# Vision-transformer block on one core: a token's place in the tiles goes from c*99+p to 2p+c

## The chip, the cores and the metric

The kernel runs on one core of a Trainium2 chip. The metric is the device time of one execution in microseconds, the median of three runs: 1737.85 us before the change (1737.76 to 1738.62). TensorE (PE), VectorE (DVE), ScalarE (ACT), GpSimd (POOL) and SyncE (SP) each run a program of their own and meet at semaphores. SP computes nothing: it issues most of the transfers, in order, and a transfer that has to wait for a semaphore holds up those behind it.

## The reference, cut to what matters

128 images of 224x224x3 become 196 patch tokens each (with four shifted copies), one class token stands ahead of them, and one block of attention and a quantised linear layer follow. All is float32.

```python
h = _L0_tok_ref(x, L0_tok_W, L0_tok_b)                   # (128, 196, 192)
h = jnp.concatenate([broadcast(cls_tok), h], axis=1)     # (128, 197, 192)
h = h + _L0_attn_ref(_layernorm(h), Wq, Wk, Wv, Wo, ...) # 6 heads of 32, softmax over 197 keys
h = h + _L0_ffn_ref(_layernorm(h), weight_t, bias)       # round to int8 steps, 192x192 product
return h
```

Attention mixes the tokens of an image without regard to their order; the other steps treat each token for itself. So the order in which tokens lie in a tile is free, as long as loads and store agree on it and the padding is left out.

## The kernel before

It has two stages. The first (`build_tokens`, up to about 420 us) embeds the patches, measures each token for the layer norm and stores two scratch tensors in DRAM, `h_dram` (the tokens, the residual) and `xn_dram` (the normalised tokens), each 128 x 198 x 192: 197 tokens and one row of zeros as padding (TP = 198 = 2 x TC, TC = 99).

The second stage (`build_attention`) takes the images one after the other. An image's 198 rows lie in a tile as 99 partitions by 2 halves by 192 columns. Before, half c of partition p holds token c*99+p; the padding, row 197, is partition 98 of half 1, which the value product (`kk = NTOK - TC`) and the padding's score row leave out.

Each engine's program is written out by hand in `step(i)`: at step i it works on image i+5 (transposing the normalised tokens, `f`), on the pair of images two or three ahead (query and key projections, `p`), on i+1 (scores and row maxima, `a`), i (transposed scores and exponentials, `b`), i-1 (values, `c`), i-2 (output projection and residual, `e`), i-3 (quantising, `g`) and i-4 (linear layer and store, `k`). Steps -5 to 11 and 120 to 131 are written out, and 108 steps in between run as a loop of six steps (MOD = 6): 18 passes, with a jump back between them on every engine.

What SP issues in one step, in its order: the two loads of normalised tokens for image i+7 (`load_xn`, lines 768 to 770: all 192 columns, and columns 128 to 191 a second time, into `xn_in`, which has 256 columns per half); the copies from SBUF to SBUF that stack high and low parts of queries and keys for the score product (`stack`, line 762: in odd steps nine into `q_st` and `k_st`, in even steps three into `k_st`), behind waits for ACT's and DVE's parts; the store of image i-4 (lines 825 and 826: 99 rows of half 0, 98 rows of half 1); the load of the residual of image i-1 (`h_in`, line 830); and, behind a wait for ACT, the row maxima of image i+1 into `q_st` (line 752). TensorE waits before the first score product of an image (`score`, lines 903 to 908) for all stacked copies of its pair. VectorE adds the residual in line 1257 after a wait for line 830's load, and writes `y` in line 1239 after a wait for the store of the image two before.

Of the kernel before, what the change touches and what calls it, by code (L numbers as in the profile page):

```python
# [21 lines left out]
NTOK = G * G + 1  # L22
TP = NTOK + 1
TC = TP // 2
# [602 lines left out]
def build_attention(nc, s):  # L627
# [17 lines left out]
    def tile(name, shape, dt=F32):  # L645
        return sb(name, shape, dt, attention)
# [25 lines left out]
    h_in = tile("h_in", [TC, NS, 2, D])  # L672
# [6 lines left out]
    y = tile("y", [TC, NS, 2, D])  # L679
# [16 lines left out]
    y_stored = [sem(f"y_stored{i}") for i in range(MOD)]  # L696
# [25 lines left out]
    def images(eng, step):  # L722

        first, last = 2 * MOD, B - 8
        assert first % MOD == last % MOD == 0
        for i in range(-5, first):
            step(At(0, i, MOD))
        with eng.Fori(first // MOD, last // MOD) as k:
            for r in range(MOD):
                step(At(k, r, MOD))  # L730
        for i in range(last, B + 4):
            step(At(0, i, MOD))

    def pair_of(i):

        return i.plus(3 if i.r % 2 else 2)

    def leads(n):

        return n.fixed and 0 <= n.n < 2  # L740

    def stack_one(eng, image, dst, row, heads, src):

        eng.dma_start(dst[row * HD:(row + 1) * HD, 0, heads[0]:heads[1], image, :].bitcast(F32),
                      src[:, image * TP:(image + 1) * TP].bitcast(F32))\
            .then_inc(stacked[0] if image else first_stacked, 16)

    def store_max_rows(eng, a):
        if a.fixed and a.n == 0:
            eng.wait_ge(no_score_made, 1)  # L750
        eng.wait_ge(mrow_done, a.count(1, 1))
        eng.dma_start(q_st[ST:ST + 2, a.pair, :, a.two, :].bitcast(F32), max_rows[:, a.two, :].bitcast(F32))\
            .then_inc(max_landed[a.slot], 16)
# [4 lines left out]
    with nc.Block() as block:  # L758
        @block.sync
        def _(sp):  # L760
            def stack(p, dst, row, heads, src):
                sp.dma_start(dst[row * HD:(row + 1) * HD, p.pair, heads[0]:heads[1], :, :].bitcast(F32),
                             src.bitcast(F32)).then_inc(stacked[p.pair], 16)

            def load_xn(n):
                if n.reuses(NX):
                    sp.wait_ge(xt_done, n.count(1, 1 - NX))
                by_chunk = xn_dram[n.n].rearrange("(c p) d -> p c d", p=TC)
                sp.dma_start(xn_in[:, n.slot % NX, :, 0:D], by_chunk).then_inc(xn_landed[n.slot], 16)
                sp.dma_start(xn_in[:, n.slot % NX, :, D:DA + 2 * DB], by_chunk[:, :, DA:D]).then_inc(xn_landed[n.slot], 16)  # L770

            def step(i):
                f, p, a, c, k, ahead = i.plus(5), pair_of(i), i.plus(1), i.plus(-1), i.plus(-4), i.plus(7)
                if i.fixed and i.n == -5:
                    load_xn(f)
                    load_xn(f.plus(1))
                if ahead.within(B):
                    load_xn(ahead)
                q_first, q_last, k_first = (0, 4), (4, H), (0, SPLIT)
                q_rows, k_rows = slice(0, SPLIT * HD), slice(SPLIT * HD, BLOCK)  # L780
                if leads(p) and i.r % 2:
                    sp.wait_ge(qkhi_done, p.pair_count(3, 1))
                    stack_one(sp, 0, q_st, 0, q_first, qk_hi[:, 0, :])
                    stack_one(sp, 0, q_st, 1, q_first, qk_hi[:, 0, :])
                    sp.wait_ge(qklo_done, p.pair_count(3, 1))
                    stack_one(sp, 0, q_st, 2, q_first, qk_lo[:, 0, :])
                    sp.wait_ge(qkhi_done, p.pair_count(3, 2))
                    stack_one(sp, 0, q_st, 0, q_last, qk_hi[q_rows, 1, :])
                    stack_one(sp, 0, q_st, 1, q_last, qk_hi[q_rows, 1, :])
                    sp.wait_ge(qklo_done, p.pair_count(3, 2))  # L790
                    stack_one(sp, 0, q_st, 2, q_last, qk_lo[q_rows, 1, :])
                elif leads(p):
                    stack_one(sp, 1, q_st, 0, q_first, qk_hi[:, 0, :])
                    stack_one(sp, 1, q_st, 1, q_first, qk_hi[:, 0, :])
                    stack_one(sp, 1, q_st, 2, q_first, qk_lo[:, 0, :])
                    stack_one(sp, 1, q_st, 0, q_last, qk_hi[q_rows, 1, :])
                    stack_one(sp, 1, q_st, 1, q_last, qk_hi[q_rows, 1, :])
                    stack_one(sp, 1, q_st, 2, q_last, qk_lo[q_rows, 1, :])
                elif p.within(B) and i.r % 2:

                    sp.wait_ge(qkhi_done, p.pair_count(3, 1))
                    stack(p, q_st, 0, q_first, qk_hi[:, 0, :])
                    stack(p, q_st, 1, q_first, qk_hi[:, 0, :])
                    sp.wait_ge(qklo_done, p.pair_count(3, 1))
                    stack(p, q_st, 2, q_first, qk_lo[:, 0, :])
                    sp.wait_ge(qkhi_done, p.pair_count(3, 2))
                    stack(p, q_st, 0, q_last, qk_hi[q_rows, 1, :])
                    stack(p, q_st, 1, q_last, qk_hi[q_rows, 1, :])  # L810
                    stack(p, k_st, 0, k_first, qk_hi[k_rows, 1, :])
                    stack(p, k_st, 2, k_first, qk_hi[k_rows, 1, :])
                    sp.wait_ge(qklo_done, p.pair_count(3, 2))
                    stack(p, q_st, 2, q_last, qk_lo[q_rows, 1, :])
                    stack(p, k_st, 1, k_first, qk_lo[k_rows, 1, :])
                elif p.within(B):
                    k_last = (SPLIT, H)
                    sp.wait_ge(qkhi_done, p.pair_count(3, 3))
                    stack(p, k_st, 0, k_last, qk_hi[:, 2, :])
                    stack(p, k_st, 2, k_last, qk_hi[:, 2, :])  # L820
                    sp.wait_ge(qklo_done, p.pair_count(3, 3))
                    stack(p, k_st, 1, k_last, qk_lo[:, 2, :])
                if k.within(B):
                    sp.wait_ge(y_done, k.count(1, 1))
                    sp.dma_start(out[k.n, 0:TC, :], y[:, k.two, 0, :]).then_inc(y_stored[k.slot], 16)
                    sp.dma_start(out[k.n, TC:NTOK, :], y[0:NTOK - TC, k.two, 1, :]).then_inc(y_stored[k.slot], 16)
                if c.within(B):
                    if c.reuses(NS):
                        sp.wait_ge(h1_done, c.count(1, 1 - NS))
                    sp.dma_start(h_in[:, c.two, :, :], h_dram[c.n].rearrange("(c p) d -> p c d", p=TC))\  # L830
                        .then_inc(h_landed[c.slot], 16)
                if a.within(B) and not leads(a):
                    store_max_rows(sp, a)

            sp.dma_start(h_dram[:, (G - 1) * G + 1:NTOK, :], h_t[:, LAST, 0:G, :]).then_inc(last_row_stored, 16)
            sp.wait_ge(last_row_xn, G - EARLY)
            sp.dma_start(xn_dram[:, (G - 1) * G + 1 + EARLY:NTOK, :], xn_t[:, EARLY:G, :]).then_inc(last_row_stored, 16)
            sp.wait_ge(last_row_stored, 32)
            sp.wait_ge(pads_stored, 32)
            sp.wait_ge(cls_landed, 32)  # L840
            for p in range(2):
                sp.wait_ge(h_stored[p], 16 * (G // 2 - p))
            sp.wait_ge(xn_stored, 16 * G)
            sp.wait_ge(early_stored, 16)
            images(sp, step)
            for n in range(B - MOD, B):
                sp.wait_ge(y_stored[n % MOD], 32 * (n // MOD + 1))
# [585 lines left out]
```

## Time and profile before

| | before |
|---|---|
| median of 3 runs (lowest to highest) | 1737.85 us (1737.76 to 1738.62) |
| span of the profiled execution | 1736.1 us |
| busy: TensorE, its weight loads, VectorE | 95%, 87%, 85% of the span |
| busy: GpSimd, ScalarE | 53%, 44% |
| DMA queue of SP's copies | 65.4% of 16 engines' span, 204690 packets |

The profile gives one execution, seen by the hardware profiler; its span runs from the first to the last instruction. Its own time outside the span is not recorded, so the median of the runs stands beside it: 1.75 us lie around the span. A DMA packet is one piece moved by one of the 16 DMA engines. An entry "issue" in a list of waits is idle time for which the profile shows no releaser.

### The profile page before, as it was taken

What the parts mean: (1) busy time and instruction counts of PE and PEld (TensorE: products, weight loads), DVE (VectorE), ACT (ScalarE), POOL (GpSimd) and SP (SyncE); (2) the same over time, 40 slices, a digit from 0 to 9 for tenths busy, and PEclk for the clock granted to TensorE, in tenths of its full rate; (3) what the DMA queues carried; (4) which work ended last, traced back from release to release, by engine and by line L of the source; (5) the groups of instructions that cost most, each with busy time, mean ns of one, the idle gap of its engine ahead of it and who ended that gap; (6) DMA issues with size and microseconds to landing.
All of it is one profiled execution on the core that took longest, in us unless ns stands there. A gap on an engine that the chain in (4) does not pass through costs nothing.

```text
span 1736.1 us, 53274 instructions
## 1 busy us (share of the span) xinstructions
PE 1655.0 (95%) x16368; PEld 1504.7 (87%) x16368; DVE 1471.9 (85%) x3906; ACT 759.4 (44%) x1751; POOL 925.9 (53%) x1911
## 2 busy tenths in 40 slices
PE   4999999996699999999999999999999999999996
PEld 4999999996588888888888888888888888888884
DVE  7888888895388988888888888888888888888885
ACT  2000000001265555556565555655556555555653
POOL 3353544536055655555555565556555555555555
PEclk9999999998699999999999999999999999999998
DMA  9999999973777778787887878877787878878771
GB/s 299 265 306 297 314 290 308 314 257 143 123 140 151 142 146 146 148 147 138 148 149 149 145 139 147 150 146 143 143 147 146 150 138 147 147 150 145 139 119 33
DMA packets 216158, 303.66 MB, mean 175 GB/s; under 512 B 47776, under 2 KB 205011, under 8 KB 205988
## 3 DMA queue, kind: packets, MB, share of 16 engines
q1 hardware_dynamic: 204690, 227.17, 65.4%
q10 hardware_dynamic: 7426, 39.47, 7.8%
q0 software_dynamic: 3984, 36.28, 5.3%
q8 instruction: 32, 0.52, 0.1%
q14 instruction: 26, 0.21, 0.0%
HBM read 126.54 MB, written 58.29 MB: 106 GB/s over the span
## 4 chain that ended last, share of the span: by engine, by line
PE 50%; DVE 8%; POOL 7%; issue 7%; DMA 2%; SPq 1%; ACT 0%; ACTq 0%; POOLq 0%; DVEq 0%
PE bank L874 9%; PE o_bank L932 8%; PE bank L922 6%; PE bank L908 6%; PE bank L895 5%; PE bank L883 5%; PE o_bank L855 3%; PE o_bank L951 2%; PE bank L855 2%; PE o_bank L960 2%; POOL ln L163 2%; DVE neg_max L1193 2%; PE bank L1007 2%; DMA k_st<-qk_lo 2%; POOL qx L1369 2%
## 5 line engine op out<-in xcount | busy, mean ns | idle before, releaser
L1093 ACT ACTIVATE probs<-bank 99x396 f32<-99x396 f32 x768 | 381.8, 497 | 217.7 <-PE bank L922 217.4
L1336 POOL TENSOR_TENSOR key_sum<-probs 99x396 f32<-99x396 f32 x256 | 227.4, 888 | 433.5 <-ACT probs L1093 284.5
L1193 DVE TENSOR_REDUCE neg_max<-bank 99x2 f32<-99x394 f32 x768 | 419.4, 560 | 16.4 <-PE bank L908 12.3
L340 PE MATMUL bank<-e_t,xt 128*128 128x192 f32 x2352 | 389.0, 329 | 25.2 <-DVE xt L448 21.5
L340 PEld LDWEIGHTS bank<-e_t,xt 128*128 128x128 f32 x2352 | 387.5, 192 | 26.4 <-DVE xt L448 26.2
L922 PE MATMUL bank<-q_st,k_st 99*99 99x198 f32 x1536 | 280.6, 264 | 5.7 <-DMA q_st<-max_rows 2.9
L908 PE MATMUL bank<-k_st,q_st 96*99 96x198 f32 x1536 | 275.6, 275 | 10.1 <-DMA k_st<-qk_lo 4.1
L448 DVE STREAM_TRANSPOSE xt<-x_t 128x256 f32<-128x256 f32 x588 | 214.9, 416 | 46.0 <-PE bank L340 44.6
L922 PEld LDWEIGHTS bank<-q_st,k_st 99*99 99x99 f32 x1536 | 208.0, 167 | 50.5 <-issue 42.5
L908 PEld LDWEIGHTS bank<-k_st,q_st 96*99 96x99 f32 x1536 | 193.3, 167 | 26.8 <-issue 12.6
L932 PE MATMUL o_bank<-probs,vals 99*32 99x198 f32 (+1 forms) x3072 | 199.0, 337 | 0.0
L1087 ACT ACTIVATE o_t<-o_bank 128x396 f32<-128x396 f32 x128 | 64.1, 501 | 234.9 <-PE o_bank L951 234.9
L932 PEld LDWEIGHTS o_bank<-probs,vals 99*32 99x32 f32 (+1 forms) x3072 | 113.6, 110 | 47.3 <-ACT probs L1093 0.2
L951 PE MATMUL o_bank<-key_sum,pick 99*32 99x198 f32 x1536 | 151.9, 332 | 0.0
L1369 POOL TENSOR_SCALAR qx<-h,ln 99x192 f32<-99x192 f32 x256 | 126.4, 501 | 40.1 <-POOL ln L163 40.1
L1348 POOL TENSOR_TENSOR hb<-h,ffn_bias 99x384 f32<-99x384 f32 x128 | 129.4, 1011 | 3.7 <-DVE h L1257 3.7
L349 ACT ACTIVATE ffn_w_bf<-ffn_raw 96x384 bf16<-96x384 int8 x1 | 0.5, 522 | 294.8 <-DVE xt L448 294.8
L163 POOL TENSOR_TENSOR ln<-ln,minus_half 99x2 f32<-99x2 f32 x128 | 116.0, 906 | 23.1 <-POOL ln L162 23.1
L1210 DVE TENSOR_TENSOR qk_lo<-bank,qk_hi 128x396 fp32r<-128x396 f32 x192 | 108.3, 564 | 19.4 <-ACT qk_hi L1102 18.4
L895 PE MATMUL bank<-wo_hi,a_mix 128*99 128x192 f32 x512 | 120.3, 253 | 0.0
L895 PE MATMUL bank<-wo_lo,a_mix 128*99 128x192 f32 x512 | 120.2, 253 | 0.0
L1102 ACT ACTIVATE qk_hi<-bank 128x396 fp32r<-128x396 f32 x192 | 96.1, 501 | 49.9 <-PE bank L874 43.2
(134 smaller groups left out, 3593.0 us busy)
## 6 DMA issues: line engine op xcount, KB each, us to landing
x_t<-in_x_dram SPq DMA_DIRECT2D x26, 1344.0 KB, 21.9
x_t<-in_x_dram ACTq DMA_DIRECT2D x26, 1344.0 KB, 23.1
q_st<-qk_hi SPq DMA_DIRECT2D x126, 198.0 KB, 4.4
k_st<-qk_hi SPq DMA_DIRECT2D x126, 198.0 KB, 4.4
xn_in<-xn_scratch SPq DMA_DIRECT2D x128, 148.5 KB
h_in<-h_scratch SPq DMA_DIRECT2D x128, 148.5 KB
h_scratch<-h_t POOLq DMA_DIRECT2D x13, 1344.0 KB, 17.2
xn_scratch<-xn_t POOLq DMA_DIRECT2D x13, 1344.0 KB, 8.0
```

The source lines that it names most:

```text
L340: last = pe.matmul(token_bank(p)[:, 0:D], xt[:, p, c // 3, c % 3, :], e_t[:, row_kind(t), col, c // 3, c % 3, :], start=c == 0, stop=c == 5)
L448: last = nc.vector.transpose(xt[:, p, :, c, :].rearrange("p m (g b) -> p g m b", b=32), pix[:, c])
L874: last = pe.matmul(wide(bank, BLOCK), weights[:, Q:K + 1, :].rearrange("p w n -> p (w n)")[:, cols], inputs, start=i == 0, stop=i == len(p ...
L895: last = pe.matmul(bank[0:TC, c * D:(c + 1) * D], inputs, weights, start=i == 0, stop=i == len(pairs) - 1)
L908: last = pe.matmul(S_BANK[h % 2][0:TC, c * TP:(c + 1) * TP], q_st[0:ST, n.pair, h, n.two, c * TC:(c + 1) * TC], k_st[0:ST, n.pair, h, n.tw ...
L922: last = pe.matmul(T_BANK[0:TC, c * TP:(c + 1) * TP], k_st[:, n.pair, h, n.two, c * TC:(c + 1) * TC], q_st[:, n.pair, h, n.two, :], start= ...
L932: pe.matmul(o_bank[at % 4 * HD:(at % 4 + 1) * HD, 0, col:col + TP], vals[0:kk, n.two, kc, h, :], probs[0:kk, n.two, h, kc, :], start=kc == ...
L951: last = pe.matmul(o_bank[to:to + HD, 0, TP:2 * TP], pick[:, j, :], key_sum[:, n.two, HEAD_AT[side * HG + j], :], start=j == 0, stop=j == ...
L1093: nc.scalar.activation(probs[:, n.two, h, :, :], wide(T_BANK, TC), ACT.Exp).then_inc(exp_done, 1)
L1193: nc.vector.tensor_reduce(out=neg_max[:, n.two, :, h], in_=wide(S_BANK[h % 2], TC)[:, :, 0:NTOK], axis=AX_X, op=ALU.max, negate=True).then ...
L1336: nc.gpsimd.tensor_tensor(key_sum[:, b.two, heads, :], probs[:, b.two, heads, 0, :], probs[:, b.two, heads, 1, :], ALU.add).then_inc(pool_ ...
L1369: nc.gpsimd.tensor_scalar(qx[:, e.two, cc, :], h1[:, e.two, cc, :], v[7][:, cc:cc + 1], v[6][:, cc:cc + 1], ALU.add, ALU.mult).then_inc(ln ...
```

## The change

Half c of partition p now holds token 2p+c. Row 197, the padding, stays at partition 98 of half 1. The two tokens of a partition are neighbours in DRAM: 2 x 768 = 1536 bytes. The load of the residual and the store therefore name one run of 384 columns per partition; token 196 (partition 98, half 0) has a store of its own. The load of normalised tokens reads neighbouring rows, into a tile whose halves are 256 columns apart.

```diff
-                by_chunk = xn_dram[n.n].rearrange("(c p) d -> p c d", p=TC)
+                by_chunk = xn_dram[n.n].rearrange("(p c) d -> p c d", c=2)
...
-                    sp.dma_start(out[k.n, 0:TC, :], y[:, k.two, 0, :]).then_inc(y_stored[k.slot], 16)
-                    sp.dma_start(out[k.n, TC:NTOK, :], y[0:NTOK - TC, k.two, 1, :]).then_inc(y_stored[k.slot], 16)
+                    sp.dma_start(out[k.n, 0:NTOK - 1, :].rearrange("(p c) d -> p c d", c=2), y[0:TC - 1, k.two, :, :])\
+                        .then_inc(y_stored[k.slot], 16)
+                    sp.dma_start(out[k.n, NTOK - 1:NTOK, :], y[TC - 1:TC, k.two, 0, :]).then_inc(y_stored[k.slot], 16)
...
-                    sp.dma_start(h_in[:, c.two, :, :], h_dram[c.n].rearrange("(c p) d -> p c d", p=TC))\
+                    sp.dma_start(h_in[:, c.two, :, :], h_dram[c.n].rearrange("(p c) d -> p c d", c=2))\
                         .then_inc(h_landed[c.slot], 16)
```

No instruction changes its place. SP's program of before, from the k_st copies of an even step to the first copy of the odd step behind it (partitions x pieces x columns of the destination; `out_dram` is the result):

```order
L762 DMA k_st<-qk_lo 32x4x396
L825 DMA out_dram<-y 99x192
L826 DMA out_dram<-y 98x192
L830 DMA h_in<-h_scratch 99x2x192
L752 DMA q_st<-max_rows 2x6x198
L769 DMA xn_in<-xn_scratch 99x2x192
L770 DMA xn_in<-xn_scratch 99x2x64
L762 DMA q_st<-qk_hi 32x4x396 x2
```

Here the residual's load and both stores name runs of 192 columns. The same place in the changed kernel:

```order
L762 DMA k_st<-qk_lo 32x4x396
L825 DMA out_dram<-y 98x384
L827 DMA out_dram<-y 1x192
L831 DMA h_in<-h_scratch 99x384
L752 DMA q_st<-max_rows 2x6x198
L769 DMA xn_in<-xn_scratch 99x2x192
L770 DMA xn_in<-xn_scratch 99x2x64
L762 DMA q_st<-qk_hi 32x4x396 x2
```

The two stores and the residual's load have other shapes; the loads of normalised tokens keep theirs, and the order is the same.

## Rows read from the trace of the kernel before

**Rows 1.** Windows: us, busy us of PE, PEld, DVE, ACT, POOL, clock, DMA share, GB/s
```profile
430.00:485.00 55.00, 39.34 (x261) 33.83 (x262) 23.23 (x55) 16.76 (x37) 3.55 (x4) 0.66 0.69 123
485.00:1650.00 1165.00, 1154.69 (x13011) 1025.07 (x13011) 1033.05 (x2674) 685.49 (x1604) 680.99 (x1428) 1.00 0.79 146
```

**Rows 2.** Head of the page
```profile
span 1736.1 us, 53274 instructions
```

**Rows 3.** Waits of PEld from 485 to 1650 us: us, times, longest
```profile
PEld bank L908 <- issue: 12.6, 33, 0.5
PEld bank L908 <- DMA k_st<-qk_lo: 0.4, 1, 0.4
```

**Rows 4.** Timeline of PEld at 871 and 881 us: start, us, idle before
```profile
871.75 0.34 PEld L908 LDWEIGHTS bank<-k_st,q_st 96*99 96x99 f32 x3 [0.46 <-issue]
...
880.99 0.44 PEld L908 LDWEIGHTS bank<-k_st,q_st 96*99 96x99 f32 x4 [0.19 <-issue]
```

**Rows 5.** Timeline of SP, 869.8 to 876.4 us: start, us of issue
```profile
870.40 0.35 SPq L826 DMA_DIRECT2D out_dram<-y  x1
870.94 0.33 SPq L830 DMA_DIRECT2D h_in<-h_scratch  x1
872.08 0.67 SPq L752 DMA_DIRECT2D q_st<-max_rows  x1
873.46 0.33 SPq L769 DMA_DIRECT2D xn_in<-xn_scratch  x1
873.97 0.30 SPq L770 DMA_DIRECT2D xn_in<-xn_scratch  x1
874.39 1.26 SPq L762 DMA_DIRECT2D k_st<-qk_hi  x2
875.70 0.61 SPq L762 DMA_DIRECT2D k_st<-qk_lo  x1
```

**Rows 6.** DMA view, 873.9 to 875.4 us, while the token load runs
```profile
DMA packets 202, 0.14 MB, mean 97 GB/s; under 512 B 19, under 2 KB 202, under 8 KB 202
q1 hardware_dynamic: 202, 0.14, 40.8%
```

**Rows 7.** DMA view, 1733.5 to 1736.1 us, the last store
```profile
DMA packets 222, 0.15 MB, mean 58 GB/s; under 512 B 25, under 2 KB 222, under 8 KB 222
q1 hardware_dynamic: 222, 0.15, 20.1%
```

**Rows 8.** DMA view, 421.9 to 424.7 us, a store of 4608-byte rows
```profile
DMA packets 144, 0.59 MB, mean 211 GB/s; under 512 B 16, under 2 KB 16, under 8 KB 144
q1 hardware_dynamic: 144, 0.59, 52.4%
```

**Rows 9.** DMA view, 870 to 876 us: busy tenths in 40 slices
```profile
DMA  9999999999999999877777651000059016777789
```

**Rows 10.** Waits of all engines over the span
```profile
DVE h L1257 <- PE bank L895: 23.1, 79, 0.9
```

**Rows 11.** Waits of SP over the span
```profile
SPq L752 <- ACT max_rows L1087: 303.6, 124, 5.4
SPq L847 <- DMA out_dram<-y: 1.2, 1, 1.2
```

**Rows 12.** Views of two one-row loads: ns of issue min/median/max
```profile
L358 ACTq DMA_DIRECT2D an_row<-in_L_attn_anchors_dram x1: 228/228/228, 1.5 to 1.5; - x1
...
L360 ACTq DMA_DIRECT2D lam_row<-in_L_attn_lam_dram x1: 266/266/266, 1.8 to 1.8; - x1
```

**Rows 13.** Timeline of SP at the end
```profile
1733.58 0.30 SPq L825 DMA_DIRECT2D out_dram<-y  x1
1733.91 0.36 SPq L826 DMA_DIRECT2D out_dram<-y  x1
```

**Rows 14.** Page, sections 2 and 3
```profile
DMA packets 216158, 303.66 MB, mean 175 GB/s; under 512 B 47776, under 2 KB 205011, under 8 KB 205988
...
q1 hardware_dynamic: 204690, 227.17, 65.4%
```

## The prediction

> **What bounds the kernel now.** I read the windows first: from 485 to 1650 us, where nearly all images are worked on, TensorE is busy 1154.69 of 1165 us at a granted clock of 1.00, the level of 2.4 GHz [rows 1]. That leaves 10.3 us of idle time in two thirds of the span [rows 2], and the change leaves every TensorE instruction as it is. In the same rows the DMA engines are busy 0.79, so the second question is whether some transfer lands late for TensorE. The waits of its weight loads answer that [rows 3]: of the waits before the first score matmul (L908), 0.4 us are put down to the DMA into k_st and 12.6 us, in 33 waits, to "issue".
>
> Two rows of one loop turn tell these 33 apart [rows 4]. The wait of 0.46 us at 871.75 comes where TensorE's own program jumps back; with 18 passes there are 17 such turns, 17 x 0.46 = 7.8 us. The other 16 waits hold 12.6 - 7.8 = 4.8 us. Of these 880.99 is one: SP issued the last k_st piece at 875.70 [rows 5] and the score matmul started 5.3 us later, 0.19 us late. It happens once a pass, because SP's jump back (872.08 + 0.67 to 873.46) delays the token load and with it the three k_st copies behind it. So all that a faster or slower DMA could give or take in the body hangs on how soon the k_st copies of a pass's first image land: at most 4.8 + 0.4 = 5.2 us to win.
>
> **The change, part by part.**
>
> *Load of normalised tokens (xn_in).* The destination keeps 256 columns per half, so a partition's two halves do not join: the program's row stays 99x2x192, with the second copy at 99x2x64. The same 198 + 198 pieces move, from neighbouring rows of DRAM instead of rows 99 apart. This is the only one of the three that stands ahead of the k_st copies on SP at the place that counts [rows 5]. Its cost after is not shown by any row, so I bound it. In the stretch in which its large pieces run, 40.8% x 16 x 1.5 us = 9.8 us for 202 packets, 48 ns each [rows 6]; the pieces of the last store, the same 768 bytes, cost 20.1% x 16 x 2.6 = 8.4 us for 222 packets, 38 ns [rows 7]. If the new order brought the load down to 38 ns, it would be done 198 x 10 / 16 = 0.13 us sooner, a little more if fewer than 16 engines share it; I call that 0.2 us. If it brought the pieces up to 70 ns (my estimate below for a piece of twice the size, the dearest near row), it would be 198 x 22 / 16 = 0.27 us later. I take zero, the same pieces at the same price.
>
> *Load of the residual (h_in) and the store.* 198 pieces become 99, and 99 + 98 become 98 + 1. The price of a joined piece is an estimate from two rows: 768 bytes cost at most 8.4 us / 197 = 42 ns if the 25 small packets are free [rows 7], and 4608 bytes 52.4% x 16 x 2.8 / 128 = 183 ns [rows 8]. The line through both gives 70 ns for 1536 bytes, so a pair saves 84 - 70 = 14 ns, and an image 197 x 14 = 2.8 us of engine time, 0.17 us on each of 16 engines. Nothing waits for that in the body. The DMA engines stand idle between the end of store, residual and maxima and the start of the token load: four slices of 0.15 us at about 873.8 to 874.4 read 0 [rows 9]. What ends sooner ahead of that gap only widens it. VectorE's addition of the residual waits, where it waits, for TensorE (23.1 us, 79 times), and the list of waits has no entry that names the transfer [rows 10]. So both edits count zero in the body; if that cover were gone, 0.17 us an image over some 120 images, 20 us, would be the most, but TensorE's idle time of 10.3 us caps it and the 5.2 us above are the only part of it that waits for transfers. SP's wait for the maxima (L752, 303.6 us in 124 waits [rows 11]) also hides the issue time of the single-row store: 0.35 us for the row it replaces (870.40 [rows 5]), 0.23 and 0.27 us for two one-row copies of the start [rows 12]; before the maxima at 872.08 SP has 872.08 - 871.27 = 0.8 us [rows 5].
>
> The Trainium skill, "DMA: Bandwidth & Descriptors" (Specifications), names 512 bytes as the size from which a transfer runs at line rate, and by that joining 768-byte pieces gains nothing, 0 instead of 14 ns a pair. The rows disagree in part: 768 bytes in 42 ns is 18 bytes per ns, 4608 in 183 ns is 25. By either the body's sum is zero.
>
> *The end.* After VectorE's last result SP issues the two stores at 1733.58 and 1733.91 [rows 13] and waits 1.2 us for them [rows 11]. Engine time falls from 8.4 us to 98 x 70 + 42 ns = 6.9 us, and the second transfer is one piece instead of 98. I take 0.2 us off; it can't be over 1.2 us, and a single row that lands late costs at most about the 0.35 us of an issue.
>
> The same page ("Why a DMA increments its semaphore by 16 and not by 1") says that a copy from SP runs on the largest number of engines up to 16 that divides the outer size on both sides, each posting one completion. The 25 small packets beside 197 pieces agree: 11 for 99 rows and 14 for 98. By it the new store uses 14 engines and the single row one, with 7 or 8 pieces on the fullest instead of 16, and the token load stays on 11; the 0.2 us stands.
>
> *The start of the attention stage.* From 430 to 485 us TensorE is busy 39.3 of 55 us [rows 1]; the token loads there keep their pieces. I take zero, with half a us to either side.
>
> **Sum.** Body 0, start 0, end -0.2: the span goes from 1736.1 [rows 2] to 1735.9 us. The median of the runs shown, 1737.85 us, is 1.75 us above the span of the profiled execution; I keep that: 1737.6 us. 0.2% of it, about what a measurement here tells from no change, is 3.5 us.
>
> **Rivals.** (1) Faster: the token load gets cheaper with neighbouring rows, the k_st copies land sooner, and the 16 late starts shrink. For it: the load's pieces do cost 10 ns more than the store's. Against it: a 0.2 us gain takes at most 16 x 0.2 = 3.2 us, which is 1734.4 us; only the whole 5.2 us, 1732.4 us, is clearly beyond 3.5 us. I set this case at 1733.9 us, chance 0.09. (2) Slower: the token load gets dearer, because its engines now read a closer stretch of DRAM and get in each other's way; k_st then lands later in the first image of each of 18 passes, where nothing is left to hide it. At 0.27 us later, 18 x 0.27 = 4.9 us, 1742.5 us; it decides from 3.5 / 18 = 0.19 us on. Against it: the load's pieces and bytes are the same, and the first 768-byte pieces are slow before as well. Chance 0.07. (3) The single row disturbs: a store of one row per image that lands late, or start and end shift by more than I count; the y buffer is needed again only two images later, so it is worth a us or two, 1739 us, chance 0.06. (4) My forecast, which includes that one of the three transfers doesn't get larger pieces at all: 1737.6 us, chance 0.78, its own range 1736.5 to 1738.7.
>
> Faster by over 0.2%: 0.09; slower by over 0.2%: 0.07; within: 0.84. The range goes from 1734.4 (all of a 0.2 us earlier landing) to 1740.5 us (a landing 0.16 us later, 18 x 0.16 = 2.9 us), and leaves out about 0.14.
>
> **What would show it.** Right: DMA packets fall by 128 x (197 + 10) = 26,496; the queue of SP's copies falls from 65.4% by 128 x 2.8 / (16 x 1736) = 1.3 points [rows 14]; TensorE's idle time from 485 to 1650 us stays within 3 us of 10.3; the 33 waits before L908 stay at about 12.6 us. Wrong: that sum moves by several us with the copies into k_st landing other than 5.3 us after issue; a wait of VectorE for h_in, or of SP for a slot of its queue; matmuls of other length.

## The result and the profile after

The changed kernel takes 1803.11 us (median of four runs, 1800.19 to 1807.71) against 1737.8 us before (four runs too): the ratio is 1.0383 with a 95% interval from 1.0366 to 1.0399. The time is 65 us longer, far outside the predicted range.

The head of the profile after, and the windows (columns as in [rows 1]):

```profile
span 1800.9 us, 53274 instructions
```
```profile
485.00:1650.00 1165.00, 1100.42 (x12270) 969.23 (x12269) 976.27 (x2526) 647.88 (x1517) 649.37 (x1349) 1.00 0.77 138
```

In the same 1165 us TensorE is busy 1100.42 us, 54.3 less than in [rows 1], at the same granted clock of 1.00 (2.4 GHz). The instructions are as many as in [rows 2]. So TensorE waits; its waits in this stretch (us, times, longest) say for what. First its products before and after, then its weight loads after, to be held against the 12.6 us in 33 waits of [rows 3]:

```profile
PE bank L908 <- DMA k_st<-qk_lo: 0.8, 4, 0.3
```
```profile
PE bank L909 <- DMA k_st<-qk_lo: 54.8, 55, 1.5
PEld bank L909 <- issue: 73.0, 70, 1.8
```

L909 is L908 of before, the first score product. Over the whole span the page puts it so, before and after (busy us, mean ns, then idle before it and what ended most of that):

```profile
L908 PE MATMUL bank<-k_st,q_st 96*99 96x198 f32 x1536 | 275.6, 275 | 10.1 <-DMA k_st<-qk_lo 4.1
```
```profile
L909 PE MATMUL bank<-k_st,q_st 96*99 96x198 f32 x1536 | 276.1, 275 | 66.3 <-DMA k_st<-qk_lo 60.9
```

The product itself is as long as before (275 ns). Before, the idle time ahead of it was 10.1 us over the span; the 56.2 us more are most of the 64.8 us by which the span grew. The place is the one the prediction watched, the landing of the k_st copies, but late in 55 steps of the window, about 1 us each on average; the window has 56 even steps. To see why they land late, SP's timeline in an even step at a loop turn (start, us of issue), the counterpart of [rows 5]:

```profile
953.58 0.32 SPq L831 DMA_DIRECT2D h_in<-h_scratch  x1
954.45 0.73 SPq L752 DMA_DIRECT2D q_st<-max_rows  x1
955.93 0.97 SPq L769 DMA_DIRECT2D xn_in<-xn_scratch  x1
957.09 0.84 SPq L770 DMA_DIRECT2D xn_in<-xn_scratch  x1
958.06 1.28 SPq L762 DMA_DIRECT2D k_st<-qk_hi  x2
959.38 0.60 SPq L762 DMA_DIRECT2D k_st<-qk_lo  x1
```

Every issue but two is about as long as before. The two token loads take 0.97 and 0.84 us of SP where they took 0.33 and 0.30. From the maxima to the last k_st copy it is 954.45 to 959.38, 4.93 us; in [rows 5] it was 872.08 to 875.70, 3.62 us. What follows, in the chain of waits and in the timelines of TensorE's product and weight load:

```profile
959.38 5.41 DMA k_st<-qk_lo
```
```profile
964.91 0.60 PE L909 MATMUL bank<-k_st,q_st 96*99 96x198 f32 x4 [1.48 <-DMA k_st<-qk_lo]
```
```profile
964.91 0.43 PEld L909 LDWEIGHTS bank<-k_st,q_st 96*99 96x99 f32 x4 [1.72 <-issue]
```

The product starts 5.5 us after the copy's issue, before 5.3 us, so the landing is nearly what it was; but the copy is issued 1.3 us later, and the weight load waits 1.72 us in place of 0.19 [rows 4]. That the long issue holds for all 128 images is seen in the view of the tile, before and after (ns of issue, min/median/max; first and last start):

```profile
L769 SPq DMA_DIRECT2D xn_in<-xn_scratch x128: 292/337/619, 424.8 to 1637.9; - x128
L770 SPq DMA_DIRECT2D xn_in<-xn_scratch x128: 297/297/730, 425.1 to 1638.3; - x128
```
```profile
L769 SPq DMA_DIRECT2D xn_in<-xn_scratch x128: 811/936/1040, 421.4 to 1702.6; - x128
L770 SPq DMA_DIRECT2D xn_in<-xn_scratch x128: 811/866/1273, 422.5 to 1703.6; - x128
```

By the medians (337 and 297 ns before) the two loads together take 1.17 us more of SP. The program as built shows what changed in them. Source and destination of the first load, as [step in elements, count] for each dimension:

```
before  source [192, 99] [19008, 2] [1, 192]   destination [1536, 99] [256, 2] [1, 192]   marked
after   source [192, 198] [1, 1] [1, 192]      destination [1536, 99] [256, 2] [1, 192]   not marked
```

Rows 2p and 2p+1 for all p lie at one distance, so the source is written as one dimension of 198 rows; the destination, with a hole of 64 columns between its 192s, stays 99 x 2. The lists of instructions ahead of the prediction give the destination's shape alone, and there nothing had changed. The "mark" is one that the built program calls "precooked"; in the attention stage every copy of SP whose two sides have the same counts carries it, and none whose sides differ. By the medians of the traces, the marked copies there issue in 0.23 to 0.43 us (h_in, the stores, the token load of before), the others in 0.59 to 0.94 us (stack copies, described as 128 rows against 32 x 4, or 64 against 32 x 2; the maxima, 12 against 2 x 6; the token load of after). Mark and like description always go together here, so no run tells them apart.

The rest went as the change says. Packets, against [rows 14]:

```profile
DMA packets 189662, 303.65 MB, mean 169 GB/s; under 512 B 46496, under 2 KB 178515, under 8 KB 179492
...
q1 hardware_dynamic: 178194, 227.17, 64.6%
```

### The profile page after: what moved, and what is told of

Read it like the earlier page. It is cut to its first block, busy times and chain, and to the rows that moved or that the text cites. A ratio compares the mean times of both kernels' runs of the same rounds, so it can differ in the third digit from the quotient of the medians.

```text
span 1800.9 us, 53274 instructions
## 1 busy us (share of the span) xinstructions
PE 1660.1 (92%) x16368; PEld 1502.5 (83%) x16368; DVE 1473.2 (82%) x3906; ACT 759.7 (42%) x1751; POOL 933.3 (52%) x1911
## 2 busy tenths in 40 slices
DMA packets 189662, 303.65 MB, mean 169 GB/s; under 512 B 46496, under 2 KB 178515, under 8 KB 179492
## 3 DMA queue, kind: packets, MB, share of 16 engines
q1 hardware_dynamic: 178194, 227.17, 64.6%
## 4 chain that ended last, share of the span: by engine, by line
PE 36%; DMA 18%; SPq 13%; issue 4%; DVE 2%; POOL 2%; ACT 1%; ACTq 1%; POOLq 0%; DVEq 0%
DMA k_st<-qk_lo 17%; PE bank L875 7%; PE o_bank L933 5%; PE bank L909 5%; PE bank L923 5%; SPq L762 4%; SPq L769 3%; PE bank L884 3%; SPq L770 3%; PE bank L896 3%; SPq L752 2%; PE bank L856 2%; PE o_bank L856 2%; PE o_bank L961 2%; PE o_bank L952 1%
## 5 line engine op out<-in xcount | busy, mean ns | idle before, releaser
L909 PE MATMUL bank<-k_st,q_st 96*99 96x198 f32 x1536 | 276.1, 275 | 66.3 <-DMA k_st<-qk_lo 60.9
L909 PEld LDWEIGHTS bank<-k_st,q_st 96*99 96x99 f32 x1536 | 193.5, 167 | 91.5 <-issue 75.2
L1370 POOL TENSOR_SCALAR qx<-h,ln 99x192 f32<-99x192 f32 x256 | 143.1, 566 | 40.1 <-POOL ln L163 40.1
L1201 DVE TENSOR_TENSOR key_sum<-probs 99x396 f32<-99x396 f32 x128 | 74.5, 582 | 62.2 <-ACT probs L1094 62.2
```

Source lines behind the costliest of these rows:

```text
L909: last = pe.matmul(S_BANK[h % 2][0:TC, c * TP:(c + 1) * TP], q_st[0:ST, n.pair, h, n.two, c * TC:(c + 1) * TC], k_st[0:ST, n.pair, h, n.tw ...
L1370: nc.gpsimd.tensor_scalar(qx[:, e.two, cc, :], h1[:, e.two, cc, :], v[7][:, cc:cc + 1], v[6][:, cc:cc + 1], ALU.add, ALU.mult).then_inc(ln ...
```

## The experiments

The first four ask which part does it, and whether it is the place on SP. First the changed kernel with the token load in its old order (residual and store stay changed):

```diff
-                by_chunk = xn_dram[n.n].rearrange("(p c) d -> p c d", c=2)
+                by_chunk = xn_dram[n.n].rearrange("(c p) d -> p c d", p=TC)
```

> The changed kernel with the load of normalised tokens alone put back to rows 99 apart (residual and store keep the new order, so the residual is added to other tokens). Theory 1 (issue): after the change SP takes 0.94 + 0.87 us instead of 0.34 + 0.30 us to issue the two token loads, because the source now reads as 198 rows and the destination as 99 x 2; the k_st copies behind them leave 1.2 us later and TensorE waits. With the old source the issue is back at 0.34 + 0.30 us and the time at that of before, 1735 to 1740 us. Theory 2 (joined pieces): the 1536-byte pieces or the single-row store hold up SP's ring; the time stays at 1795 to 1805 us.

Measured: 1737.17 us, ratio 1.0009 [0.9999, 1.0018]. Its tile view and its page:

```profile
L769 SPq DMA_DIRECT2D xn_in<-xn_scratch x128: 292/337/622, 424.9 to 1639.1; - x128
```
```profile
L909 PE MATMUL bank<-k_st,q_st 96*99 96x198 f32 x1536 | 275.7, 275 | 9.8 <-issue 3.9
```

So the larger pieces of the residual and the store, with the single-row store, come to between 0 and 3 us of loss, which can't be told from nothing. The converse, the kernel before with the token load alone in the new order:

```diff
-                by_chunk = xn_dram[n.n].rearrange("(c p) d -> p c d", p=TC)
+                by_chunk = xn_dram[n.n].rearrange("(p c) d -> p c d", c=2)
```

> The kernel before with the new order in the load of normalised tokens alone (residual and store in the old order, so the residual is added to other tokens). Theory 1 (issue): 1798 to 1808 us, with 0.9 us of issue for each of the two loads. Theory 2 (joined pieces): 1735 to 1740 us. Theory 3 (the reads of neighbouring rows are slow on the DMA engines): also about 1803 us, but with the load's packets dearer than the 48 ns of before and the issue unchanged.

Measured: 1795.63 us, 1.0341 [1.0324, 1.0358]. The long issue and the wait come with this one line, and with them 60 of the 65 us; its interval does not meet that of the whole change, and where the last few us come from is not shown:

```profile
L769 SPq DMA_DIRECT2D xn_in<-xn_scratch x128: 811/927/1036, 425.0 to 1698.0; - x128
```
```profile
L908 PE MATMUL bank<-k_st,q_st 96*99 96x198 f32 x1536 | 276.5, 275 | 58.0 <-DMA k_st<-qk_lo 52.8
```

Next, the changed kernel with the token load moved ahead of the wait for the maxima, so that the k_st copies no longer stand behind it in SP's program:

```diff
-                if ahead.within(B):
-                    load_xn(ahead)
                 q_first, q_last, k_first = (0, 4), (4, H), (0, SPLIT)
...
                         .then_inc(h_landed[c.slot], 16)
+                if ahead.within(B):
+                    load_xn(ahead)
                 if a.within(B) and not leads(a):
```

> The changed kernel with SP's two token loads moved from the head of a step to behind the residual's load, ahead of the row maxima, where SP waits for ScalarE anyway. Same loads, same issue time. Theory 1 (issue): the k_st copies no longer stand behind the loads, so the 60 us go: 1733 to 1742 us, although the issue stays at 0.9 us each. Theory 3 (slow reads): the loads still run on the same DMA engines, right ahead of the copies, and at most half of the loss goes: 1765 us or more.

> The kernel before with the same move of the token loads. Theory 1 (issue): the copies of every image leave about 1 us sooner than before, and the up to 5.2 us of late starts that the trace of before shows ahead of the first score product go: 1731 to 1736 us. If the copies' landing is set by the DMA engines and not by when SP issues them: 1736 to 1740 us, no change.

The second is the same move in the kernel before. Measured: 1750.2 us, 1.0089 [1.0072, 1.0106], and 1742.4 us, 1.0036 [1.0022, 1.005]; both are above what was expected. The loads of the moved changed kernel still take 0.93 and 0.88 us, yet most of the 65 us is gone: length of issue costs only where something late stands behind it. What is left goes at least in part with something that I had not expected: in both, TensorE waits for the maxima. The waits of its weight loads, moved changed kernel first, then the moved kernel before:

```profile
PEld bank L923 <- DMA q_st<-max_rows: 23.2, 59, 1.4
```
```profile
PEld bank L922 <- DMA q_st<-max_rows: 39.7, 59, 2.4
```

The same view of the kernel before, where the token load comes behind the maxima, and then a piece of the chain of waits in the moved kernel before (start, us):

```profile
PEld bank L922 <- DMA q_st<-max_rows: 0.6, 2, 0.3
```
```profile
1289.76 3.85 DMA q_st<-max_rows
```

ScalarE had ended the maxima at 1289.70, SP issued them at once, and their 9.3 KB landed 3.85 us after the issue. So here a small copy issued right behind the token load lands late, and the expectation for the kernel before failed on that; that the load's packets ahead of it are the reason is argued, not shown. In the moved changed kernel it is the issue again (ScalarE, then SP):

```profile
957.33 0.31 ACT L1088 ACTIVATE max_rows<-o_bank 12x198 fp32r<-12x198 f32 x1
```
```profile
957.96 0.87 SPq L770 DMA_DIRECT2D xn_in<-xn_scratch  x1
958.94 0.72 SPq L752 DMA_DIRECT2D q_st<-max_rows  x1
```

The maxima were ready at 957.64, but SP was at the token loads until 958.83 and issued them 1.3 us late; TensorE's wait for them ends at 961.10, 2.2 us after that issue. The k_st copies of this kernel, too, are still late in 18 steps of the window, 6.1 us in all.

Is it SP's time, or the order of the rows in DRAM? One kernel adds SP time without touching the token load, by two copies of 12 pieces of 64 bytes, described as 12 against 2 x 6:

```diff
...
+                for j in range(2):
+                    few = xn_dram[n.n, 0:12, 16 * j:16 * j + 16].rearrange("(p c) d -> p c d", c=6)
+                    sp.dma_start(spare[:, n.slot % NX, j, :, :], few).then_inc(spare_landed[n.slot], 16)
...
```

> The kernel before, all rows in the old order, with two tiny copies more behind each pair of token loads: 12 pieces of 64 bytes each from the token scratch into a spare tile, source 12 rows, destination 2 x 6. They move next to nothing and cost SP an estimated 0.6 to 0.7 us of issue each, since the maxima's copy of the same shape takes 0.67 us. Theory 1 (issue time of SP ahead of the k_st copies): 1.2 to 1.6 us of delay per image, 1795 to 1825 us. Theory 3 (slow reads) and theory 2 (joined pieces), which need the data: 1735 to 1740 us.

Measured: 1855.6 us, 1.0689 [1.0674, 1.0705]. The tile of the two copies, and TensorE's waits:

```profile
L778 SPq DMA_DIRECT2D spare<-xn_scratch x256: 610/650/789, 425.4 to 1755.4; - x128
```
```profile
PE bank L917 <- DMA k_st<-qk_lo: 79.2, 54, 2.0
```

Each copy moves 768 bytes and holds SP for 0.65 us, twice as long as the first token load in the old order with its 198 pieces of 768 bytes. That confirms the place and the kind of the cost. The size was missed: 118 us, above the range of the expectation. Part of the excess is TensorE's clock. A piece of its timeline, and two stretches right behind it (columns as in [rows 1]):

```profile
920.34 0.97 PE L917 MATMUL bank<-k_st,q_st 96*99 96x198 f32 x4 [1.91 <-DMA k_st<-qk_lo]
```
```profile
920.40:923.80 3.40, 3.40 (x13) 3.35 (x14) 1.04 (x2) 0.67 (x2) 1.89 (x4) 0.50 0.24 62
923.80:929.00 5.20, 5.20 (x69) 4.40 (x69) 4.22 (x10) 2.06 (x5) 0.00 (x0) 1.00 0.85 128
```

After a wait of 1.91 us for k_st the granted clock is 0.50, the level of 1.2 GHz, for 3.4 us. The window has 13 such stretches, each behind a wait of 1.6 to 1.9 us for k_st; the steps that hold them take 13.4 to 13.7 us, while loop turns without one take 11.9 to 12.2. At about 1.5 us each they are some 20 of the 118 us. (The changed kernel has two such stretches in the window, 3 us by the same estimate.)

Half the dose, the kernel before with only the first of the two loads in the new order:

```diff
+                near = xn_dram[n.n].rearrange("(p c) d -> p c d", c=2)
-                sp.dma_start(xn_in[:, n.slot % NX, :, 0:D], by_chunk).then_inc(xn_landed[n.slot], 16)
+                sp.dma_start(xn_in[:, n.slot % NX, :, 0:D], near).then_inc(xn_landed[n.slot], 16)
```

> The kernel before with only the first of the two token loads in the new order; the 64-column copy keeps the old one (so the doubled columns belong to other tokens). Theory 1 (issue): one load at 0.93 us, the other at 0.30 us, the copies leave 0.6 us later instead of 1.2 us. The trace of before has about 0.4 us of room in two of three even steps and none at a loop turn, so less than half of the loss: 1750 to 1770 us. A cost per byte or per piece read from neighbouring rows would be three quarters of the loss (768 of 1024 bytes a row), about 1780 us.

Measured: 1767.16 us, 1.0172 [1.0157, 1.0187], half the loss for one long issue (the second load's median is 374 ns):

```profile
L770 SPq DMA_DIRECT2D xn_in<-xn_scratch x128: 836/931/1034, 424.5 to 1667.2; - x128
```

Then near rows with a source that can't be joined: partition p reads rows p and p+1 (so most rows are read twice, others not at all).

```diff
+                rows_in = xn_dram[n.n].rearrange("(c p) d -> p c d", p=TC)
+                by_chunk = bass.AP(rows_in.tensor, rows_in.offset, [[D, TC], [D, 2], [1, D]])
```

> The kernel before with token loads that read rows p and p+1 into partition p (neighbouring rows, so most tokens are read twice and the upper half of an image not at all), which keeps the source at 99 x 2 as the destination is. Theory 1 (issue, from the differing description of the two sides): issue stays at 0.34 + 0.30 us, 1735 to 1740 us. Theory 3 (reads of neighbouring rows are slow): 1780 us or more.

Measured: 1736.86 us, 1.0001 [0.9992, 1.001], with an issue as in the old order (the second load's median is 297 ns):

```profile
L770 SPq DMA_DIRECT2D xn_in<-xn_scratch x128: 292/337/556, 424.0 to 1637.7; - x128
```

And the changed kernel's own rows 2p+c with sides that agree, by one pair of copies for each half:

```diff
+                for c in range(2):
+                    sp.dma_start(xn_in[:, n.slot % NX, c, 0:D], by_chunk[:, c, :]).then_inc(xn_landed[n.slot], 16)
+                    sp.dma_start(xn_in[:, n.slot % NX, c, D:DA + 2 * DB], by_chunk[:, c, DA:D]).then_inc(xn_landed[n.slot], 16)
...
-                    pe.wait_ge(xn_landed[f.slot], f.landed(32))
+                    pe.wait_ge(xn_landed[f.slot], f.landed(64))
```

> The changed kernel, with its token load split by halves into four copies, 99 x 192 and 99 x 64 for each half: the same rows 2p+c to the same places, but source and destination described alike. Theory (SP's issue is long where the two sides are described with different counts): each copy issues in 0.30 to 0.35 us, so four of them with 0.2 us between take 1.9 us against 2.0 us for the two long ones and 0.8 us before; the k_st copies leave 1.1 us later than before, 64 even steps lose 0.7 to 0.8 us each, and the time is about 1785 us (1775 to 1797). Rival (rows at the new distance are what takes SP longer): each of the four takes 0.5 us or more, 2.6 us in all, and the time is 1830 us or more.

Measured: 1789.91 us, 1.0301 [1.0285, 1.0317]. The issue of each copy, and the wait that is left:

```profile
L770 SPq DMA_DIRECT2D xn_in<-xn_scratch x256: 292/319/609, 423.3 to 1689.2; - x128
L771 SPq DMA_DIRECT2D xn_in<-xn_scratch x256: 296/297/1120, 423.7 to 1689.6; - x128
```
```profile
PE bank L910 <- DMA k_st<-qk_lo: 43.9, 56, 1.4
```

The same rows, each copy taking every second one, issue in 0.32 and 0.30 us once both sides are described alike; the copies carry the mark. The rival, that the distance of rows costs SP its time, is out by these two runs. But four issues with their gaps hold the k_st copies up nearly as long as two long ones, and the time says so.

Last, a version that takes the token loads off this path: loads for two images together in even steps, ahead of the wait for the maxima, and none in odd steps, where k_st copies follow (line numbers of the kernel before; the changed kernel got the same edit).

```diff
-                if ahead.within(B):
+                if i.fixed and i.n == -5:
                     load_xn(ahead)
...
+                if i.r % 2 == 0:
+                    for n in (ahead, ahead.plus(1)):
+                        if n.within(B):
+                            load_xn(n)
```

> The kernel before, rows in the old order, with the token loads of two images issued together in even steps, between the residual's load and the maxima, where SP waits 4 us for ScalarE, and none in odd steps. The k_st and q_st copies then stand directly behind the maxima in both kinds of step, and in odd steps nothing new stands ahead of the maxima. If the late starts before the first score product come from SP's issue order alone: the 5.2 us of them go, 1730 to 1734 us (0.1 to 0.3% under before). If the maxima of even steps land late behind two token loads, as those of odd steps did with one load ahead: 1738 to 1745 us.

> The changed kernel with the token loads of two images issued together in even steps, ahead of the maxima, and none in odd steps. Issue stays at about 0.93 + 0.87 us a load pair, so four loads take some 4.2 us with the gaps; between the residual's load and the maxima of an even step the version of before with this order has 950.57 to 955.28 us, 4.7 us. Theory 1 (issue): the long issue is hidden in that wait, all of the loss goes, and the time is that of the old row order with the same placing, 1727 to 1735 us. If the maxima are pushed past the room they have: 1740 us or more. If the joined pieces are worth anything once issue is out of the way, it comes out under 1727 us.

> The kernel before with the token loads of two images issued together in even steps, ahead of the wait for the maxima, again, now on one chip with the same edit of the changed kernel. Theory: 1730 us, ratio 0.996; TensorE's waits for k_st copies gone but for the 17 loop turns.

> The changed kernel with the same pairing, on the same chip. Theory: with the k_st copies no longer behind the token loads, issue time is all hidden and larger pieces are worth nothing: the same as the paired kernel before within 0.1% (1730 us). Rival: the joined load still costs something in the even steps, where four issues of 0.9 us stand ahead of the maxima: 4 us more, 1734 us, with waits for q_st<-max_rows in the list.

Measured for the kernel before with paired loads: 1729.91 us, 0.9957 [0.9942, 0.9971], and on another chip 1732.44 us, 0.9972 [0.9961, 0.9984]. For the changed kernel with paired loads: 1734.37 us, 0.9993 [0.9983, 1.0002], and beside the second run of the former 1733.44 us, 0.9976 [0.9967, 0.9985]. In the one comparison on the same chip the two paired versions can't be told apart: taken off the path, the long issues cost nothing and the joined pieces bring nothing that shows above some 3 us. (The first two runs, each on a chip of its own against the kernel before there, differ by 0.4%; why is not known.) SP in the paired kernel before, second run:

```profile
949.38 0.33 SPq L830 DMA_DIRECT2D h_in<-h_scratch  x1
949.91 0.33 SPq L769 DMA_DIRECT2D xn_in<-xn_scratch  x1
950.43 0.30 SPq L770 DMA_DIRECT2D xn_in<-xn_scratch  x1
950.92 0.30 SPq L769 DMA_DIRECT2D xn_in<-xn_scratch  x1
951.40 0.30 SPq L770 DMA_DIRECT2D xn_in<-xn_scratch  x1
954.41 0.67 SPq L752 DMA_DIRECT2D q_st<-max_rows  x1
```

The four loads fill time in which SP waited for the maxima anyway; the next issue is 954.41, 2.7 us after the last of them ends. TensorE's waits for the score products, from 485 to 1650 us, in its weight loads and in its products (the same in both runs):

```profile
PEld bank L912 <- issue: 8.3, 19, 0.5
PE bank L912 <- issue: 3.9, 17, 0.3
```

Against [rows 3], 12.6 us in 33 waits have become 8.3 in 19, of which 17 are the loop's turns; no wait for k_st is left. This version, rows in the old order and loads paired, is faster than both kernels, by 0.3 to 0.4% against the one before.

## Why the prediction was wrong

**The step that failed** is "*Load of normalised tokens*", where it says "I take zero, the same pieces at the same price". It priced the pieces on the DMA engines, from 0.13 us sooner to 0.27 us later, and left out the other price of a transfer, SP's time to issue it. For the single-row store the prediction did weigh an issue; for the load that it had itself named as the one ahead of the k_st copies it did not. That term is 1.17 us of issue an image. In the window 55 even steps lose 54.8 us by it, 1.0 us each; at that rate 64 even steps, one for each pair of images, lose 64 of the 65 us. The prediction's own sign of a miss was a landing other than 5.3 us after issue; the landing held (5.5 us) and the issue moved.

**The sign could be read before.** [Rows 5] show the maxima, 9.3 KB, issued in 0.67 us and k_st copies in 0.61, but the token load in 0.33 and 0.30. Issue time there doesn't follow bytes; it goes with whether the two sides are described alike. The diff had made the sides of one load unlike.

**The bound on the loss was too small.** The slower rival had the right place, k_st landing later, and counted 18 late steps because only those had no room. But the room of the other even steps had to be held against the delay. Here is the step behind the loop turn of [rows 5], before (SP, then TensorE), and the like step after:

```profile
894.93 0.60 SPq L762 DMA_DIRECT2D k_st<-qk_lo  x1
```
```profile
900.57 0.60 PE L908 MATMUL bank<-k_st,q_st 96*99 96x198 f32 x4
```
```profile
985.41 0.61 PE L909 MATMUL bank<-k_st,q_st 96*99 96x198 f32 x4 [0.73 <-DMA k_st<-qk_lo]
```

Before, the product starts 5.64 us after the copy's issue and waits for nothing; at the loop turn it starts 5.29 us after it. So the room was about 0.35 us. After, the copies are issued 1.3 us later in such a step as well, and the product waits 0.73 us there against 1.48 us at the loop turn. Nearly every even step pays, each the delay less its room. The kernel with four copies agrees: 4.57 us from maxima to last k_st copy at a loop turn, 0.95 later than before, and a mean wait of 43.9 / 56 = 0.78 us.

**What was right.** The pieces of the token load keep about their price. While it runs after, at 957.5 to 958.6 and at 904.3 to 905.4 us, and in a second stretch of before, 864.0 to 864.9 us:

```profile
q1 hardware_dynamic: 208, 0.15, 42.1%
q1 hardware_dynamic: 209, 0.15, 54.6%
```
```profile
q1 hardware_dynamic: 194, 0.14, 55.9%
```

42.1% x 16 x 1.1 us / 208 is 36 ns a packet and 54.6% x 16 x 1.1 / 209 is 46 ns after; before, it is 48 ns in [rows 6] and 55.9% x 16 x 0.9 / 194 = 42 ns. Stretches of one kernel differ by as much as the two kernels do, so the gain that the faster rival counted on is not shown. Packets fell by 216,158 - 189,662 = 26,496, the number predicted. The residual and the store count zero, as far as the first experiment can tell. VectorE's waits ahead of its addition of the residual are for TensorE still, 21.6 us in 73 times (23.1 in 79 in [rows 10]), and the list has no wait for the transfer. The single-row store issues in 235 ns, between the two of [rows 12]:

```profile
L827 SPq DMA_DIRECT2D out_dram<-y x128: 227/235/276, 503.3 to 1798.9; - x128
```

The end of the program costs what it cost: SP's last wait is 1.2 us, as in [rows 11].

```profile
SPq L848 <- DMA out_dram<-y: 1.2, 1, 1.2
```

The 0.2 us predicted there can't be told from nothing. What the paired kernel before won, 5.3 us on the one chip and 7.4 on the other by the medians, is near the "at most 5.2 us to win" behind the landing of k_st, the second above it.

**A second price that was off.** The load on SP's queue fell from 65.4% to 64.6%, 0.8 points where 1.3 were predicted, but only because the span grew: 65.4% x 16 x 1736.1 us is 18.17 ms of engine time, 64.6% x 16 x 1800.9 is 18.61 ms, more and not less. The first experiment has the joined pieces without the new token load:

```profile
q1 hardware_dynamic: 178194, 227.17, 64.8%
```

With its span of 1738.6 us that is 18.03 ms, 0.14 ms or about 1.1 us an image less than before, where the prediction had 2.8 us. By this one comparison a joined piece saves less than half of the 14 ns a pair that the line through two rows gave. No engine waits for it, so the time does not show it.

**What stays open.** What SP does in the additional 0.6 us of a copy is not shown, nor whether the description or the mark decides; the runs show with which copies it comes. A single load of rows 2p+c whose source stays at 99 x 2 was not tried. Of the loss with the two small copies, the clock explains about 20 us of 118; the rest is still more than was expected.

## What to carry to other kernels

A transfer has two prices here: the packets' time on the DMA engines, and SP's time to issue it, by which everything behind it in SP's program leaves later. When an edit changes an access pattern, compare the dimensions of both sides after joining, not the pieces alone; here a layout that is more regular on one side only made the issue nearly three times as long. And hold the delay of a late transfer against the room of every step, not only of those that are late already; loads that nobody awaits soon belong where the queue idles anyway.

## What was not expected of the hardware

- Two transfers of equal pieces and bytes take SP 0.34 or 0.94 us to issue, by their description and the mark that goes with it; a copy of 768 bytes described unlike takes 0.65 us, one of 198 x 768 bytes described alike 0.34 us.
- A small copy right behind the token load on the same queue lands 3.85 us after its issue (moved kernel before), late enough that TensorE waits for it in 59 weight loads of the window.
- TensorE's granted clock fell from 1.00 to 0.50 (2.4 to 1.2 GHz) for 3.4 us at a time behind waits of 1.6 to 1.9 us for k_st, 13 times in the window of the kernel with two small copies more, so its time grew by more than the waits.
